# Twelve gate and up steps inside the preparation of weights, their products in a ring of 13 tiles

## The reference

```python
xn = layernorm(x)
# FFN branch: every operand is rounded blockwise (16 along the last dim) to FP4 values times a scale
q  = lambda a: grid_round(a / scale) * scale        # scale = max|block| / 6
h  = silu(q(x) @ q(w_gate).T) * (q(x) @ q(w_up).T)  # inner size 1408; the FFN's x is xn as well
f  = q(h) @ q(w_down).T                             # back to 512
# state-space branch
a  = xn + ssm_scan(rmsnorm(xn, scale1), A, B, C, D)   # 16 states per channel, along the tokens
a  = a + gelu(rmsnorm(a, scale2) @ w1 + b1) @ w2 + b2 # inner size 2048
out = x + a + f
```

## Time and profile before

| | us |
|---|---|
| median of 3 runs | 3091.5 |
| the profiled execution, first to last instruction | 3092.0 |
| its TensorE, busy | 2991.3 |
| its VectorE, busy | 2177.3 |
| its GpSimd, busy | 1519.8 |
| its ScalarE, busy | 1146.4 |

### The profile page before, as it was taken

How to read it: one execution, slowest core, us unless ns; L and a number is a source line. 1 busy time by engine, 2 the same in 40 slices (tenths; PEclk the granted TensorE clock), 3 DMA queues, 4 the chain that set the end, 5 groups by cost and what they waited for, 6 DMA issues and landing times.

```text
span 3092.0 us, 43985 instructions
## 1 busy us (share of the span) xinstructions
PE 2991.3 (97%) x14573; PEld 2417.7 (78%) x14573; DVE 2177.3 (70%) x4451; ACT 1146.4 (37%) x1934; POOL 1519.8 (49%) x1417
## 2 busy tenths in 40 slices
PE   5799999999999999999999899999999999999999
PEld 3678888888887777777777788788888888888887
DVE  7798898887877677777777676776665656565622
ACT  5445656644453343433433343222222222222220
POOL 7556666665555555554555235423444434353513
PEclk9999999999999999999999999999999999999999
DMA  4133343346766666666643458777777676768541
GB/s 126 48 86 93 118 118 107 97 133 180 191 175 171 162 168 163 154 162 172 166 120 99 126 134 203 170 178 205 203 179 205 174 214 168 206 165 218 150 127 48
DMA packets 965425, 469.89 MB, mean 152 GB/s; under 512 B 688080, under 2 KB 816336, under 8 KB 962640
## 3 DMA queue, kind: packets, MB, share of 16 engines
q1 hardware_dynamic: 965200, 467.08, 58.0%
HBM read 330.06 MB, written 136.87 MB: 151 GB/s over the span
## 4 chain that ended last, share of the span: by engine, by line
PE 66%; DVE 18%; issue 5%; POOL 5%; DMA 2%; ACT 2%; SPq 1%; DVEq 0%; POOLq 0%; ACTq 0%
PE bank L1225 16%; PE bank L1203 15%; PE bank L1029 14%; PE bank L1051 7%; PE bank L1152 4%; PE bank L1168 4%; DVE qs L1349 3%; POOL qa L2124 2%; DVE qa L1366 2%; PE bank L1092 2%; DVE qs L1360 2%; DVE qa L1322 2%; POOL qa L2118 1%; DVE qb L1374 1%; PE bank L999 1%
## 5 line engine op out<-in xcount | busy, mean ns | idle before, releaser
L1029 PE MATMUL bank<-XT,Wu 128*128 128x512 f32 (+1 forms) x2148 | 515.5, 389 | 16.1 <-DVE sg L1314 15.8
L1029 PE MATMUL bank<-XT,Wg 128*128 128x512 f32 (+1 forms) x2148 | 522.8, 392 | 7.3 <-DVE Wd L1381 7.3
L1051 PE MATMUL bank<-Wd,HT 128*128 128x512 f32 x2112 | 515.5, 393 | 6.6 <-POOL HT L2132 5.3
L1029 PEld LDWEIGHTS bank<-XT,Wu 128*128 128x128 f32 x2148 | 400.9, 190 | 106.7 <-issue 25.9
L2124 POOL TENSOR_TENSOR qa<-qb,qs 128x512 f32<-128x512 f32 (+2 forms) x277 | 308.5, 1114 | 342.3 <-DVE qb L1374 337.8
L1051 PEld LDWEIGHTS bank<-Wd,HT 128*128 128x128 f32 x2112 | 391.8, 188 | 106.2 <-issue 15.4
L1029 PEld LDWEIGHTS bank<-XT,Wg 128*128 128x128 f32 x2148 | 397.4, 189 | 95.9 <-DVE Wd L1381 9.4
L1225 PE MATMUL bank<-Wp,G 128*128 128x512 f32 x1536 | 388.4, 389 | 5.1 <-POOL G L2249 5.1
L1203 PE MATMUL bank<-HC,Wp 128*128 128x512 f32 x1440 | 361.7, 389 | 1.7 <-POOL WH L2242 1.7
L2132 POOL TENSOR_TENSOR HT<-qb,HT 128x512 fp32r<-128x512 f32 (+1 forms) x179 | 229.9, 1284 | 242.2 <-ACT HT L1817 242.0
L1225 PEld LDWEIGHTS bank<-Wp,G 128*128 128x128 f32 x1536 | 288.1, 188 | 66.1 <-POOL G L2249 6.3
(11 more groups left out here) (199 smaller groups left out, 4543.4 us busy)
## 6 DMA issues: line engine op xcount, KB each, us to landing
Wp<-r_A SPq DMA_DIRECT2D x336, 256.0 KB, 3.5
px<-in_L_attn_x_dram SPq DMA_DIRECT2D x128, 256.0 KB, 3.3
xin<-in_L_attn_x_dram SPq DMA_DIRECT2D x128, 256.0 KB, 3.4
sT<-r_K SPq DMA_DIRECT2D x128, 256.0 KB, 4.2
r_Z<-xin SPq DMA_DIRECT2D x64, 256.0 KB, 2.4
r_U<-ub SPq DMA_DIRECT2D x16, 1024.0 KB, 6.7
sU<-r_U SPq DMA_DIRECT2D x32, 512.0 KB, 5.1
r_Y<-sY SPq DMA_DIRECT2D x16, 1024.0 KB, 5.6
```

The lines of the kernel that those rows point to most:

```text
L1029: ins = e.matmul(bk[:, 0:n], W[wh][:, k, :], inputs(xh, w, k), start=(k == 0 and p_ == 0), stop=(k == KD - 1 and p_ == 2))
L1051: ins = e.matmul(DNB[t % 4][:], HT[hh][:, w % 2, a * P:(a + 1) * P], Wd[wh][:, f, :], start=(w == first(n) and p_ == 0), stop=(w == last(n ...
```

## The change

- `HEAD` has 38 jobs: 30 w, 8 x. x tiles 0 to 5 and the down weights stand among the gate and up weights in the order in which steps can use them.
- Steps 0 to 11 (`G` = 12) run their gate and up halves in the preparation. `HALVES` gives each of the 24 halves a turn after which it is issued: 8 to 19 without a gap, then 21, 22, 24, 25, 27, 28, 30, 31, 33 to 36. `silu` follows five, `h_mult` six iterations later.
- Their products stand in a ring of 13 tiles, `cells`, of which `sg` is the first.
- In the windows gate and up run ahead of h: window s does step `AHEAD[s]`: windows 1 to 11 do 12 to 22; of windows 12 to 33 the eleven in `LESS` (12, 14, ..., 32) do none, the others 23 to 33. From window 33 on AHEAD[s] = s as before.
- Turned weights of the preparation stand in four banks (2, 5, 7, 3), in windows in bank 7; a turn in a window no longer waits for the gate bank, nor the gate for its low part. `minus_high(m)` is issued after turn m + 1.
- `qa` has six slots in the preparation (two more in `qx`).
- No x side jobs in windows 11 to 23; side jobs of weights in windows 1 to 4 (30 to 33).
- Statistics: four tiles more in the preparation, windows 1 to 4, every other window from 10 to 36, then each to 74. Taps in windows 40 to 71 (K0 = 40), so the coefficients' heads in windows 37 to 39 and their six loads in window 34. u writes: three per window from UW0 = 76.

```diff
@@ -26,10 +26,13 @@
 NV = 32
 NB = NT // 4
 SW = 1
-K0 = 11
-UW0 = 66
+K0 = 40
+UW0 = 76
 S0 = 99
 PRE0 = 164
+G = 12
+RING = 13
+LESS = (12, 14, 16, 18, 20, 22, 24, 26, 28, 30, 32)
 BIG = 4194304.0
 FLOOR = 1.5 * BIG
 SHRINK = 1.0 - 1.5 * 2.0 ** -22
@@ -70,16 +73,41 @@
-HEAD = ([("w", i) for i in range(14)] + [("x", 0), ("x", 1)] + [("w", i) for i in range(14, 29)]
-        + [("x", 2), ("x", 3)])
+HEAD = ([("w", i) for i in range(4)] + [("x", 0), ("x", 1), ("w", 4), ("w", 5), ("x", 2), ("x", 3)]
+        + [("w", i) for i in (6, 7, 8, 9, 22, 10, 11, 23, 12, 13)] + [("x", 4), ("w", 14), ("w", 15), ("x", 5)]
+        + [("w", i) for i in (16, 17, 24, 18, 19, 25, 20, 21, 26, 27, 28, 29)] + [("x", 6), ("x", 7)])
 NJ = len(HEAD)
-
-SIDE = {1: ("w", 29), 2: ("w", 30), 3: ("w", 31), 4: ("w", 32), 5: ("x", 4), 6: ("w", 33), 7: ("x", 5), 9: ("x", 6),
-        10: ("x", 7)}
-SIDE.update({NF * i + o: ("x", 4 * i + j) for i in range(2, NB) for o, j in ((-9, 0), (-7, 1), (-3, 2), (-2, 3))})
+HPOS = {job: m for m, job in enumerate(HEAD)}
+
+
+def ahead(s):
+
+    if not SW <= s <= NW or s in LESS:
+        return None
+    w = s + G - 1 - sum(q < s for q in LESS)
+    return w if w < NW else None
+
+
+AHEAD = {s: ahead(s) for s in range(SW, NW + 1)}
+STEP = {w: s for s, w in AHEAD.items() if w is not None}
+LEAD_END = max(LESS) + 1
+WCUT = AHEAD[LEAD_END]
+
+
+def cell(w):
+
+    return w % RING if w < WCUT else 0
+
+
+CELL_BEFORE = [max((v for v in range(max(0, w - RING), w) if cell(v) == cell(w)), default=None) for w in range(NW)]
+
+SIDE = {1: ("w", 30), 2: ("w", 31), 3: ("w", 32), 4: ("w", 33), 5: ("x", 8), 7: ("x", 9), 9: ("x", 10),
+        10: ("x", 11)}
+SIDE.update({STEP[NF * i + a] - o: ("x", 4 * i + j)
+             for i in range(3, NB) for j, (a, o) in enumerate(((0, 9), (0, 7), (LAG, 6), (LAG, 5)))})
 SIDES = [SIDE[s] for s in sorted(SIDE)]
-PLACE = [q % 2 if q < 6 else (q + 1) % 2 for q in range(len(SIDES))]
+PLACE = [q % 2 for q in range(len(SIDES))]
 EARLIER = [max((p for p in range(q) if PLACE[p] == PLACE[q]), default=None) for q in range(len(SIDES))]
 SWIN = {job: s for s, job in SIDE.items()}
 JOBS = list(HEAD)
@@ -101,6 +129,18 @@
 NTH = sum(m < NJ for m in TURNS)
+def half_ready(w, b):
+
+    return 3 + max([HPOS["w", 2 * (w % NF) + b]] + [HPOS["x", 2 * n + j] for n in pairs(w) for j in range(2)])
+
+
+HALVES, _m = {}, 0
+for _w in range(G):
+    for _b in range(2):
+        _m = max(_m + 1, half_ready(_w, _b))
+        HALVES[_w, _b] = _m
+
+
 def side(s):
     return JOF[SIDE[s]] if s in SIDE else None
...
@@ -149,13 +197,13 @@
     def upto(s):
         if s < UW0:
-            return 0 if s < SW else min(s, 4) if s < 8 else min(s - 3, NT - 4)
-        return NT - 4 + min(NT, 2 * (s - UW0 + 1))
+            return 0 if s < SW else min(s, 4) if s < 8 else min(s // 2, 18) + max(0, min(s - 36, NT - 26))
+        return NT - 8 + min(NT, 3 * (s - UW0 + 1))
     return range(upto(s - 1) if s else 0, max(upto(s), upto(s - 1) if s else 0))
-TAPS = [s for s in range(K0, S0) if s - 3 not in SIDE][0:32]
+TAPS = list(range(K0, K0 + 32))
 def tap_pair(s):
@@ -262,14 +310,20 @@
         qa = sbt(actx, "qa", [P, 4, 512])
         qb = sbt(actx, "qb", [P, 2, 512])
         qs = sbt(actx, "qs", [P, 4, 2, 32])
+        with ExitStack() as qctx:
+            qx = sbt(qctx, "qx", [P, 2, 512])
         HT = [sbt(actx, f"HT{h}", [P, 2, 512], F32R) for h in range(2)]
         sg = sbt(actx, "sg", [P, 512])
         st6 = sbt(actx, "st6", [P, 2, 6])
+        with ExitStack() as nctx:
+            nI = sbt(nctx, "nI", [P, P], F32R)
         sbt(actx, "pad6", [P, 240])
         pctx = ExitStack()
         px = sbt(pctx, "px", [P, 4, D])
+        with ExitStack() as rctx:
+            cells = [sg] + [sbt(rctx, f"cell{i}", [P, 512]) for i in range(1, RING)]
         kctx = ExitStack()
         kI = sbt(kctx, "kI", [P, P + 1])
         kA = sbt(kctx, "kA", [P, 3, 4, NST])
...
@@ -441,7 +494,12 @@
             return (qb[:, m % 2] if b is None else bank[b])[:, 0:job_width(m)]
         def turned(m):
-            return (bank[(5, 7)[TPOS[m] % 2]] if m < NJ else GB)[:, 0:job_width(m)]
+            return (bank[(2, 5, 7, 3)[TPOS[m] % 4]] if m < NJ else VB)[:, 0:job_width(m)]
+
+        def quant(m):
+
+            i = quant_slot(m)
+            return qa[:, i] if i < 4 else qx[:, i - 4]
         def place(m):
             return PLACE[SIDES.index(JOBS[m])]
...
@@ -882,6 +941,13 @@
                     tile_out(side(s - 1))
                 if -40 <= k < -8:
                     decay_load(k + 40)
+                if s == LEAD_END + 1:
+                    e.wait_ge(s_src, NSOURCE[JOF["h", WCUT - 1]])
+                    for n, par in enumerate((A, B, C)):
+                        e.dma_start(kA[:, n], par.rearrange("(g p) n -> p g n", p=P)).then_inc(d_kin[n], 16)
+                    e.dma_start(kv[:, 0], col(Dv), allow_slow_non_contiguous=True).then_inc(d_kin[3], 16)
+                    e.dma_start(kv[:, 1], col(sc1), allow_slow_non_contiguous=True).then_inc(d_kin[4], 16)
+                    e.dma_start(kI[:], cst[:, C_IOTA:C_N]).then_inc(d_kin[5], 16)
                 if s == K0:
                     e.wait_ge(s_ka, 3)
                     e.dma_start(r_s.rearrange("(g p n) -> p g n", p=P, n=NST), ks[:, A8]).then_inc(d_rs, 16)
...
@@ -991,12 +1055,13 @@
                         e.wait_ge(s_ph, m + 1)
                         if TPOS[m] == 1:
                             e.wait_ge(d_cs, 16)
-                        elif m < NJ and TPOS[m] >= 3:
-                            e.wait_ge(s_lo, TPOS[m] - 2)
+                        elif TPOS[m] == 4:
+                            e.wait_ge(s_rb, 1)
+                        elif m < NJ and TPOS[m] >= 5:
+                            e.wait_ge(s_lo, TPOS[m] - 4)
                         if m >= NJ:
                             e.wait_ge(s_lo, TPOS[m] - 1)
-                            e.wait_ge(s_sg, SWIN[JOBS[m]] + 3)
-                    ins = e.matmul(turned(m)[:, k * P:(k + 1) * P], qa[:, m % 4, k * P:(k + 1) * P], ident,
+                    ins = e.matmul(turned(m)[:, k * P:(k + 1) * P], quant(m)[:, k * P:(k + 1) * P], ident,
                                    is_transpose=True, start=(k == 0 or m >= NJ), stop=(m >= NJ or k == nk - 1))
                     if k == nk - 1:
                         ins.then_inc(s_tr, 1)
...
@@ -1105,10 +1170,9 @@
             def window(s):
                 k = s - S0
-                if s < NW:
-                    if s > SW:
-                        gu_half(s, 0)
-                    gu_half(s, 1)
+                if AHEAD.get(s) is not None:
+                    gu_half(AHEAD[s], 0)
+                    gu_half(AHEAD[s], 1)
                 if side(s - 2) in TPOS:
                     turn(side(s - 2))
                 if 0 <= k < 2 * NV and k % 2:
@@ -1247,11 +1311,15 @@
             for m in range(NJ):
                 turn(m)
-                minus_high(m)
-                if 18 <= m < 26:
-                    gu_half(0, (m - 18) // 4, range((m - 18) % 4, (m - 18) % 4 + 1))
-                elif 28 <= m < 32:
-                    gu_half(1, 0, range(m - 28, m - 27))
+                for (w, b), at in HALVES.items():
+                    if at == m:
+                        gu_half(w, b)
+                if m >= 1:
+                    minus_high(m - 1)
+            minus_high(NJ - 1)
+            for (w, b), at in HALVES.items():
+                if at >= NJ:
+                    gu_half(w, b)
             for s in range(SW, NW + 1):
                 window(s)
                 if s >= PRE0 and (s - PRE0) // 3 < 4 and (s - PRE0) % 3 == 2:
...
@@ -1736,16 +1805,22 @@
                     inverse(m)
                 if m >= 2:
                     mid_b(m - 2)
-                if m == 31:
-                    h_mult(0)
+                for (w, b), at in HALVES.items():
+                    if b and at + 6 == m:
+                        h_mult(w)
                 if m < 2:
                     stats(2 * m)
                     stats(2 * m + 1)
-                if m == 1:
-                    steps.extend(batch_rsqrt(0))
-                for step in steps[0:2]:
+                if 8 <= m < 12:
+                    stats(m - 4)
+                if m in (1, 11):
+                    steps.extend(batch_rsqrt(m // 11))
+                for step in steps[0:4 if m < 5 else 2]:
                     step()
-                del steps[0:2]
+                del steps[0:4 if m < 5 else 2]
+            for w in range(G):
+                if HALVES[w, 1] + 6 >= NJ + 2:
+                    h_mult(w)
             for s in range(SW, NW + 1):
                 window(s)
                 if 0 <= s - (NW - 3) < 4:
...
@@ -1819,9 +1896,9 @@
             def silu(w):
                 n = 2 * P * len(pairs(w))
                 e.wait_ge(s_g, w + 1)
-                if w >= 1:
-                    e.wait_ge(s_src, NSOURCE[JOF["h", w - 1]])
```

(34 more changed lines are left out.)

61 lines of the change are left out of this document (29 added, 32 removed).

## The result

The changed kernel takes 3123.0 us (median of 4, 3120.7 to 3126.0) against 3091.5 of the kernel before beside it: ratio 1.0099, 95% interval [1.0084, 1.0113], 31.5 us slower. The forecast was 3096.1, with a range of 3082 to 3110. The profiled execution took 3122.0, its span 3120.2, against a span of 3092.0.

The account below looks back on a forecast made before the run. GpSimd bounds the preparation; TensorE's matmuls and the h quantization loop compete in windows. Terms: 13.4 + 0.4 - 8.5 - 14.7 = -9.4 at window 34, then +1.1 + 3.9 + 8.5 + 1 - 0.5: +4.6, 3096.1 us, range 3082 to 3110.

Parts of the forecast that it names:

- late tiles: u write stage: x tile loads four deep, three used per window, and SP's queue holding loads: +1 us (0 to 6).
- third u write: Windows 76 to 96: third write lengthens the h loop, 21 x 0.57 = 12, reserve swallows 3.5: +8.5 us (3 to 16).
- TensorE's coupling: Preparation: 3.3 us per slot against 2.56, slots 14 to 19 late, +3.5 us (0 to 7); window 1 adds +0.4.
- Preparation: Start to last job: more jobs, fewer x waits, VectorE additions, TensorE's lateness and a table load: +13.4 us, ending at 116.3.
- Windows 2 to 33: VectorE work leaves windows 2 to 11, -8.5 us; windows 12 to 33 at 7.57 plus additions, -14.7 us.
- The clock: Paired windows with and without gate and up: clock falls of about 1.7 us each, inside TensorE's idle time: 0.
- Coefficients: Heads in windows 38 and 39 instead of 9 and 10: windows 34 to 39 take +1.1 us (0 to 4).
- taps: All 32 in windows 40 to 71: 18 more at 0.27 us on TensorE, partly replacing waits: +3.9 us.
- B: Slower rival: ScalarE's queue sets the u stage in full (17) and TensorE delays the preparation by 7: 3108; chance 0.21 with D.
- A: Faster rival: later stages hide the change, u stage costs 0 to 2: 3086.6 or, partly, 3081; chance 0.24.
- C: Rival: TensorE stays at 1.2 GHz through windows 12 to 32, +67 us: 3163; chance 0.03.
- D: Rival: gate halves wait for products, so the preparation ends 12 us later; chance 0.21 together with B.

Follow-up runs that it names:

- e15: e13 with eleven gate and up steps in the preparation, a ring of 12 and ten windows without them: 2.9 us below the kernel before (0.9991).
- e13: Changed kernel, u writes behind the magnitude, eight u tile buffers loaded five writes ahead, u store issued in SP's next window: +2.1 us against the kernel before (1.0006).
- e1: Kernel before with only the u writes moved, three per window from window 76 instead of two from 66: +25.9 us (1.0082).
- e5: e1 with the coefficients and taps moved too (K0 = 40), preparation of the kernel before: +26.2 us against the kernel before (1.0081).
- e3: Kernel before with its u writes put behind the magnitude of h on ScalarE: no difference (0.9997).
- e14: e13 with the u writes ahead of the magnitude of h, as in the changed kernel: +13.7 us against the kernel before (1.0045).

## Why the prediction was wrong, step by step

Three steps failed: the price of late tiles (+1, measured 13.6), the price of the third u write (+8.5, measured 14.0), and TensorE's coupling, which was charged only up to the last job (4.8 short). The rest held, in one place by luck. The first term scaled one wait by the bytes where the slack of queue and buffers decides; the second took off a reserve that wasn't there; the third left out TensorE's own backlog after the last job.

- **Preparation, +13.4.** Right: +14.5. That GpSimd and VectorE set it is shown by the runs with eleven steps, whose last job ends at the same time. One sum in it is off by a little (40.3 + 21 x 2.56 + 6.2 - 1.2 is 99.1, not 99.2), which changes nothing.
- **TensorE's coupling and window 1, +3.5 and +0.4.** The slot of 3.3 was near (3.41, and 4.1 with two turns), but I charged it only where it held up a job of the preparation. The backlog doesn't vanish where it misses those; it was paid after the last of them, 16.9 us to window 2 and not 12.1. The table's miss says 4.8, e15 against e13 says 5.0 of the whole, and 5.4 at window 34.
- **Windows 2 to 33, -8.5 and -14.7.** Right within 1.1 each: adding up VectorE's own work at 7.57 per window holds.
- **The clock, 0.** Right. I expected a fall of the granted clock in each pair of windows without and with gate and up; it came in every second one, at a price of 1.6 to 2.3 per fall, inside idle time, and the stage is even shorter than forecast (171.9 against 173.0). The Trainium skill, "TensorE: Matmul & The Clock Gate", section "HAM oscillation — how this bites in real kernels", says that a loop whose pauses are long enough starts cold every time. The trace agrees for the six longer pauses. They cost the stage nothing, since TensorE isn't its bound.
- **Coefficients +1.1, taps +3.9.** Measured 2.5 and 2.9, but the second is right by luck. Windows 40 to 75 take 304.6 before, 302.7 with no u writes before window 76 (e1), 304.1 with all 32 taps as well (e5) and 307.5 in the changed kernel. So the taps cost 1.5. The 1.9 that e1 gives back are nearly all the late tile of window 73, a part of the price of late tiles and not of the writes: e3, which keeps the u writes there, has 8.2 in it too. The last 3.3 lie wholly in windows 64 to 75 (99.6 in e5, 102.9 in the changed kernel), while 40 to 63 are equal (204.5 in both). In windows 64 to 74 only the changed kernel still has statistics, eleven tiles of them, a term that the prediction put at nothing without a reason. The side jobs stand in other windows too; the two weren't tried apart.
- **Third u write, +8.5.** The prediction's own terms, 0.985 - 0.17 - 0.15, are 0.665 a window and 14.0 in 21 windows. It added them to 8.1 but compared the result with 8.19, which made them 0.57 and 12, and took a reserve of 3.5 off. e14's stage is 14.0 above before (8.93 a window against 8.26), each with one late transfer of about 2.5. So the terms were right, and the reserve wasn't there. It was a guess from an average, ScalarE's few waits for TensorE, and that row says that the h loop already ended last. TensorE's waits for the products of h, forecast as about 9, are 10.1 in e14.
- **Late tiles, +1 (0 to 6): the larger miss.** From e14 to the changed kernel the stage goes from 187.5 to 201.1: 13.6. I had seen a single wait of 2.56 and scaled it by the bytes; there were two, with the 1.94 in window 73. What I left out is the slack. With four buffers and three used per window, a load can start only when the previous window's writes end, and the writes of 3.07 and a landing of 4.0 don't leave much of a window; in front of the load on SP stand a round trip (16.8 us in 8) and a 1 MB store. That queue and buffers, not bandwidth, make the tiles late is shown by e13; how much each link of this chain is worth isn't.
- **Rivals.** B had both mechanisms that I had priced away, ScalarE's queue in full (17, measured 14.0) and TensorE's backlog (3.5 more, measured some 5, though after the preparation and not in it). Its 3108 lacks the late transfers. A is refuted for the changed kernel. e13, with its order and buffers put right, is where A's view of a hidden u stage holds, and even there the lag of the preparation eats the gain. C is refuted; D too: the last job came only 1.0 later than forecast.

All in all: 1.0 + 4.8 early, - 1.7 in windows 2 to 33, + 0.4 to window 76, + 18.6 in the stage of u writes, + 0.3 behind it: 23.4 beyond the 4.6 forecast, 28.0 of the 28.2 by which the spans differ. The 18.6 are 6.0 of the third write (14.0 against 8.5 less 0.5) and 12.6 of the late tiles (13.6 against 1).

## What to carry to other kernels

When a stage is compressed, list for each ring that it drains how many buffers it uses per turn of the loop and what the loader's queue waits for ahead of each load; a stall that occurs twice at two uses per turn with four buffers (4.5 us in all) is a sign that the slack is nearly gone, not a rate to be scaled: at three uses it was 16.1 in eight. Work that feeds nobody soon (here a write of u) goes behind the instruction that a loop waits for on the same engine; moving it there changed nothing in the kernel before (e3) and was worth 11.6 us in the changed one once its loads were in time. And when work is moved into a stage bound by another engine, add up the receiving engine's own total until its last item, not only where it blocks the old bound.
